# Twenty-four token blocks' normalised input transposed by 32 x 32 squares and DMA instead of by TensorE, and the squares carried through DRAM in pieces of 512 bytes

## The reference

```python
q = (x @ wq.T).reshape(b, s, H, HD)            # k and v alike; H, HD = 16, 32
q, k = apply_rope(q, inv_freq), apply_rope(k, inv_freq)
scores = einsum('bshd,bstd->bsht', q, k) / sqrt(HD)   # the heads of ONE token attend to each other
attn = einsum('bsht,bstd->bshd', softmax(scores), v).reshape(b, s, HIDDEN) @ wo.T
hidden = fwht(silu(x @ W1.T) * (x @ W3.T))            # FFN with 2048 hidden features
out = hidden @ W2.T
...
x = x + 0.5 * ffn(layernorm(x))
x = x + attn(layernorm(x))
x = x + 0.5 * ffn(layernorm(x))
```

## Time and profile before

| | |
|---|---|
| median of 3 runs | 2503.43 us (2501.75 to 2504.49) |
| the profiled execution | 2501.66 us, span 2499.8 us |
| PE busy | 2489.7 us (100%) |
| DVE busy | 2044.3 us (82%) |
| ACT busy | 530.2 us (21%) |
| POOL busy | 63.0 us (3%) |

### The profile page before, as it was taken

How to read it: one execution, slowest core, us unless ns; L and a number is a source line. 1 busy time by engine, 2 the same in 40 slices (tenths; PEclk the granted TensorE clock), 3 DMA queues, 4 the chain that set the end, 5 groups by cost and what they waited for, 6 DMA issues and landing times.

```text
span 2499.8 us, 30169 instructions
## 1 busy us (share of the span) xinstructions
PE 2489.7 (100%) x11111; PEld 2061.4 (82%) x11111; DVE 2044.3 (82%) x2602; ACT 530.2 (21%) x796; POOL 63.0 (3%) x109
## 2 busy tenths in 40 slices
PE   9999999999999999999999999999999999999999
PEld 7878888888888888888888888888888888888887
DVE  9569989699786997979969899797986979878711
ACT  3332212222121221222212122122121212211211
POOL 0030000000000000000000000000000000000000
PEclk9999999999999999999999999999999999999999
DMA  9645635455352564645635466454562545535364
GB/s 343 254 188 181 218 145 200 131 202 210 135 201 81 210 216 162 224 131 206 207 109 188 168 229 208 146 220 144 202 221 93 197 148 219 190 107 199 137 219 165
DMA packets 161172, 459.48 MB, mean 184 GB/s; under 512 B 53312, under 2 KB 82240, under 8 KB 127808
## 3 DMA queue, kind: packets, MB, share of 16 engines
q1 hardware_dynamic: 81792, 419.73, 46.0%
q10 hardware_dynamic: 79296, 38.68, 5.7%
HBM read 408.04 MB, written 38.80 MB: 179 GB/s over the span
## 4 chain that ended last, share of the span: by engine, by line
PE 90%; DVE 8%; issue 1%; DMA 0%; ACT 0%; POOL 0%; SPq 0%; DVEq 0%; ACTq 0%; POOLq 0%
PE gu L608 19%; PE gu L610 19%; PE gu L609 19%; PE acc L639 8%; PE acc L640 8%; PE acc L643 8%; PE acc L608 2%; PE acc L610 2%; PE acc L609 2%; DVE scores L1323 1%; DVE mixed L1325 1%; DVE prod L1316 1%; DVE prod L1311 1%; PE acc L736 1%; DVE gated L1584 1%
## 5 line engine op out<-in xcount | busy, mean ns | idle before, releaser
L608 PE MATMUL gu<-xt,w_up 128*128 128x512 f32 x2048 | 798.4, 390 | 0.2
L610 PE MATMUL gu<-xt,w_up 128*128 128x512 f32 x2048 | 796.8, 389 | 0.0
L609 PE MATMUL gu<-xt,w_up 128*128 128x512 f32 x2048 | 796.7, 389 | 0.0
L608 PEld LDWEIGHTS gu<-xt,w_up 128*128 128x128 f32 x2048 | 384.4, 188 | 80.7 <-issue 0.8
L609 PEld LDWEIGHTS gu<-xt,w_up 128*128 128x128 f32 x2048 | 384.4, 188 | 80.0
L610 PEld LDWEIGHTS gu<-xt,w_up 128*128 128x128 f32 x2048 | 384.4, 188 | 79.8
L1584 DVE TENSOR_TENSOR gated<-gated,gu 128x512 f32<-128x512 f32 x240 | 162.8, 679 | 239.8 <-PE gu L610 238.3
L639 PE MATMUL acc<-w_down,hid 128*128 128x512 f32 x896 | 349.6, 390 | 0.0
L640 PE MATMUL acc<-w_down,hid 128*128 128x512 f32 x896 | 348.6, 389 | 0.0
L1084 ACT ACTIVATE hid<-gated 128x512 fp32r<-128x512 f32 x240 | 152.0, 633 | 892.2 <-DVE gated L1584 882.6
L1325 DVE TENSOR_REDUCE mixed<-prod 128x64 f32<-128x1024 f32 x256 | 310.1, 1213 | 0.0
(11 more groups left out here) (144 smaller groups left out, 1946.8 us busy)
## 6 DMA issues: line engine op xcount, KB each, us to landing
w_up<-up_pairs SPq DMA_DIRECT2D x240, 1024.0 KB, 4.9
w_down<-down_pairs SPq DMA_DIRECT2D x240, 512.0 KB, 3.5
up_pairs<-w_up SPq DMA_DIRECT2D x16, 1024.0 KB, 5.1
xt<-tok ACTq DMA_DIRECT2D x176, 64.0 KB, 4.1
prod<-up_raw SPq DMA_DIRECT2D x16, 512.0 KB, 6.3
down_pairs<-w_attn SPq DMA_DIRECT2D x4, 2048.0 KB, 18.4
out<-x ACTq DMA_DIRECT2D x7, 1024.0 KB, 5.3
x<-x ACTq DMA_DIRECT2D x6, 1024.0 KB, 6.5
```

The costliest lines, as they stand in the source:

```text
L608: nc.tensor.matmul(o, w_hi, m_hi, start=first, stop=False)
L609: nc.tensor.matmul(o, w_hi, m_lo, start=False, stop=False)
L610: return nc.tensor.matmul(o, w_lo, m_hi, start=False, stop=last)
```

## The change

Block inputs take the way of the squares: the 24 early blocks are normalised in step 11, in the order of 32-feature groups that the later steps want, transposed in place on VectorE in 32 x 32 squares, kept in DRAM (`sub_squares`, step 12), brought back by 4 DMAs of 64 KB a block (steps 13 and 14), and split from SBUF (step 15). The FFN input's squares go to DRAM too (`tile_squares`, one DMA in step 10) and come back by 4 DMAs of 256 KB in step 11; its high part moves from step 14 to step 13. The attention outputs are brought back in pieces of 512 bytes into `turned`, and the split puts them in order. On ScalarE the DMA issues now stand ahead of `EXP_BEHIND`. `units_by_step` counts the new work as 1.25 a block in step 11, for 0.55 in step 13. In the prologue GpSimd's low part of the output weights waits for two ropes.

```diff
-X_STATS, X_APPLY, X_MOVE, X_SPLIT, Q_STATS, Q_APPLY = 6, 8, 10, 14, 10, 13
+X_STATS, X_APPLY, X_KEEP, X_MOVE, X_SPLIT = 6, 8, 10, 11, 13
+Q_STATS, Q_APPLY, Q_KEEP, Q_MOVE, Q_SPLIT = 10, 11, 12, 13, 15
...
-    beside[Q_APPLY] += 0.55 * len(early_subs(p + 1))
+    beside[Q_APPLY] += 1.25 * len(early_subs(p + 1))
...
             def query_key(g, between=None):
-                split_ready("q", g, 0)
+                if g in MOVED_SUBS:
+                    pe.wait_ge(s_sub_lo, MOVED_SUBS[g] + 1)
+                else:
+                    split_ready("q", g, 0)
...
             def late_gap(p):
-                output(p, 0)
-                output(p, 1)
-                if new:
-                    pe.wait_ge(s_added, SUBS * p)
-                    transpose_sub(new[0])
-                    transpose_sub(new[1])
-                output(p, 2)
-                output(p, 3)
+                for s in range(SUBS):
+                    output(p, s)
...
-                    pe.wait_ge(s_h, n0 + HT - 1)
-                    for g in early_subs(after):
-                        transpose_sub(g)
                     down_step(last, 0, False, False)
...
-            def move(p, q):
+            def keep_squares(p):
                 act.wait_ge(s_turned, SUBS * MOVED[p] + SUBS)
-                squares = turned.rearrange("p (k f c) -> p k f c", k=KT, f=QUADS)
+                act.dma_start(tile_squares, turned).then_inc(s_squares_kept, 16)
+
+            def move(p):
+
+                act.wait_ge(s_squares_kept, 16 * MOVED[p] + 16)
+                squares = tile_squares.rearrange("(q i) (k f c) -> f i k q c", q=QUADS, k=KT, f=QUADS)
                 for f in range(QUADS):
-                    act.dma_start(xt[p % 2][32 * f:32 * f + 32, 1].bitcast(FP32)[:, :, q * P:(q + 1) * P],
-                                  squares[32 * q:32 * q + 32, :, f, :]).then_inc(s_moved, 16)
+                    act.dma_start(xt[p % 2][32 * f:32 * f + 32, 1].bitcast(FP32).rearrange("p k (q c) -> p k q c", q=QUADS),
+                                  squares[f]).then_inc(s_moved, 16)
...
+            def keep_sub_squares(g):
+                act.wait_ge(s_sub_turned, MOVED_SUBS[g] + 1)
+                act.dma_start(sub_squares[new_subs(next_of(g)).index(g)], sub_normed(g)).then_inc(s_sub_kept, 16)
+
+            def move_sub(g):
+
+                later = max(early_subs(next_of(g)))
+                act.wait_ge(s_sub_kept, 16 * MOVED_SUBS[later] + 16)
+                squares = sub_squares[new_subs(next_of(g)).index(g)].rearrange("(q i) (f c) -> f i q c", q=QUADS, f=QUADS)
+                for f in range(QUADS):
+                    act.dma_start(sub_normed(g)[32 * f:32 * f + 32, :].rearrange("p (q c) -> p q c", q=QUADS),
+                                  squares[f]).then_inc(s_sub_moved, 16)
+
+            def moved_sub_high(g):
+                later = max(early_subs(next_of(g)))
+                act.wait_ge(s_sub_moved, 16 * QUADS * (MOVED_SUBS[later] + 1))
+                high = sub_split(g)[0].rearrange("p k (q j) -> p k q j", q=QUADS)
+                nc.scalar.activation(high, landed_sub(g), ACT.Copy).then_inc(s_sub_hi, 1)
...
                 act.wait_ge(s_att_kept, 16 * SUBS * (BOUNCED[i] + 1))
-                act.wait_ge(s_up_done, HT * p)
...
-                    act.dma_start(xt[(p + 1) % 2][32 * f:32 * f + 32, 1].bitcast(FP32).rearrange("p k (a j) -> p k a j", j=32),
+                    act.dma_start(turned[32 * f:32 * f + 32, :].rearrange("p (a c) -> p a c", c=P),
                                   squares[f]).then_inc(s_att_moved, 16)
...
                     nc.scalar.activation(hidden(u)[0], gated[:, u, :], ACT.Copy).then_inc(s_hid_hi, 1)
-                    if n == HT - 1 and after < NP and after not in LATE:
+                    for g in OUTPUT_KEEP.get((p, n), ()):
+                        keep_output(g)
+                    if after in MOVED and n == X_KEEP:
+                        keep_squares(after)
+                    if after in MOVED and n == X_MOVE:
+                        move(after)
+                    if after < NP and n == Q_KEEP:
                         for g in early_subs(after):
-                            sub_high(g)
+                            keep_sub_squares(g)
+                    if after < NP and Q_MOVE <= n < Q_MOVE + len(early_subs(after)):
+                        move_sub(early_subs(after)[n - Q_MOVE])
                     for g in EXP_BEHIND.get((p, n), ()):
                         exp(g)
-                    for g in OUTPUT_KEEP.get((p, n), ()):
-                        keep_output(g)
-                    if after in MOVED and X_MOVE <= n < X_MOVE + QUADS:
-                        move(after, n - X_MOVE)
                     if after in MOVED and n == X_SPLIT:
                         moved_high(after)
+                    if after < NP and n == Q_SPLIT:
+                        for g in early_subs(after):
+                            moved_sub_high(g)
...
             for m in range(4):
                 for k in range(KT):
+                    if m == O and k == 0:
+                        pool.wait_ge(s_rope, 2)
...
+            def moved_sub_low(g):
+                dve.wait_ge(s_sub_hi, MOVED_SUBS[g] + 1)
+                high, low = [part.rearrange("p k (q j) -> p k q j", q=QUADS) for part in sub_split(g)]
+                nc.vector.tensor_tensor(low, landed_sub(g), high.bitcast(FP32), ALU.subtract).then_inc(s_sub_lo, 1)
...
                         if n == Q_APPLY:
+                            if after in MOVED:
+                                dve.wait_ge(s_turned, SUBS * MOVED[after] + SUBS)
                             for s, g in enumerate(early):
-                                ln_apply(key, s, sub_normed(g), x_of(g))
+                                ln_apply(key, s, sub_normed(g).rearrange("p (f k j) -> p k f j", f=QUADS, k=KT),
+                                         x_of(g).rearrange("p (k f j) -> p k f j", f=QUADS, k=KT))
+                            for s, g in enumerate(early):
+                                dve.wait_ge(s_ln, ln_done(key, s))
+                                squares = sub_normed(g).rearrange("p (f j) -> p f j", j=32)
+                                nc.vector.transpose(squares, squares).then_inc(s_sub_turned, 1)
...
                     if n == HT - 1 and next_x:
                         for g in early:
-                            sub_low(g)
+                            moved_sub_low(g)
```

More of the change, by code:

```diff
@@ L89 @@
 UNITS = units_by_pass()
-X_STATS, X_APPLY, X_MOVE, X_SPLIT, Q_STATS, Q_APPLY = 6, 8, 10, 14, 10, 13
+X_STATS, X_APPLY, X_KEEP, X_MOVE, X_SPLIT = 6, 8, 10, 11, 13
+Q_STATS, Q_APPLY, Q_KEEP, Q_MOVE, Q_SPLIT = 10, 11, 12, 13, 15
 STEPS = HT - 1
 MOVED = {p: at for at, p in enumerate(p for p in range(2, NP) if p not in LATE)}
+MOVED_SUBS = {g: at for at, g in enumerate(g for p in range(2, NP) for g in early_subs(p))}
 QUADS = P // 32
@@ L173, in transposed @@
         elif p in LATE:
-            order += att + [("q", g, 0) for g in new[:2]] + [("x", p, k) for k in range(KT)]
+            order += att + [("x", p, k) for k in range(KT)]
         else:
-            order += [("q", g, 0) for g in early_subs(p)]
             order += [("q", g, 0) for j, g in enumerate(new[:2]) if not is_early(p, j)] + att
@@ L362, in build @@
         s_moved_lo = sem("s_moved_lo")
+        s_sub_turned = sem("s_sub_turned")
+        s_sub_kept = sem("s_sub_kept")
+        s_sub_moved = sem("s_sub_moved")
+        s_sub_hi = sem("s_sub_hi")
+        s_sub_lo = sem("s_sub_lo")
         s_att_turned = sem("s_att_turned")
@@ L458, in sub_normed, with landed_sub, landed_outputs @@
             return prod[:, 2, (j % 2) * D:(j % 2 + 1) * D]
+        def landed_sub(g):
+            return sub_normed(g).rearrange("p (q k j) -> p k q j", q=QUADS, k=KT)
+        def landed_outputs():
+            return turned.rearrange("p (a k j) -> p k a j", j=32, k=KT)
         def sub_split(g):
@@ L787, in late_gap @@
                     query_key(new[0])
-                    split_ready("q", new[1], 0)
                 pe.wait_ge(s_ln, LN_FROM["x", p] + SUBS)
@@ L952, in moved_high, with next_of @@
                     nc.scalar.activation(X[:, 0, ks, :], X[:, 1, ks, :].bitcast(FP32), ACT.Copy).then_inc(s_moved_hi, 1)
+            def next_of(g):
+                return next(p for p in range(2, NP) if g in new_subs(p))
+            def keep_sub_squares(g):
[13 more added lines that the diff above has]
+                nc.scalar.activation(high, landed_sub(g), ACT.Copy).then_inc(s_sub_hi, 1)
             def keep_output(g):
@@ L970, in moved_attention_high @@
                 act.wait_ge(s_att_moved, 16 * QUADS * (BOUNCED[WO_AT[p]] + 1))
-                X = xt[(p + 1) % 2]
+                act.wait_ge(s_up_done, HT * p)
                 for ks in (slice(0, 2), slice(2, 4)):
-                    nc.scalar.activation(X[:, 0, ks, :], X[:, 1, ks, :].bitcast(FP32), ACT.Copy).then_inc(s_att_hi, 1)
```

(11 more changed lines are left out.)

20 lines of the change are left out of this document (15 added, 5 removed).

## The result

| | before | after |
|---|---|---|
| median, 20 executions each | 2502.46 us (2501.51 to 2504.49) | 2507.41 us (2500.78 to 2511.66) |
| ratio, 95% interval | | 1.0016 [1.001, 1.0022] |
| profiled execution, span | 2501.66, 2499.8 us | 2505.99, 2504.2 us |

What follows compares the result with a forecast made beforehand. TensorE's own work was taken as the bound nearly everywhere. Pass ends 3.9 plus prologue 2.2 made 6.1 us gained, moving the median from 2503.4 to 2497.3 us; range 2494 to 2500.5, with rivals 2490.5 to 2502.7.

Steps and rivals of the forecast that it cites:

- TensorE is the bound, and two blocks' transposes are worth 0.89 us: At pass ends, removing two blocks' transposes saves TensorE 0.89 us; at most 10.7 us for all 24 blocks.
- my 0.8: Ends of passes 3, 7 and 9: 0.8 us gained each, 2.4 in all, with slightly more delay on VectorE.
- The prologue's 2.2: Prologue: with GpSimd's work behind two ropes, block 0's rope ends earlier and TensorE's wait goes, 2.2 us gained.
- Passes 1 and 10: 0: Ends of passes 1 and 10: TensorE arrives 0.45 us earlier at the normalised block and waits 0.45 longer, gaining 0.
- ScalarE ... has 79% idle, so this costs only where something late stands behind them; bounds 0 and 2.55: ScalarE's DMA issues in steps 10 to 14: cost between 0 and 2.55 us for each of passes 2 and 6.
- Pass 2 was to gain 0.77: End of pass 2: `moved_high` goes to step 13, so VectorE's 0.77 us wait for the last SiLU goes.
- A move takes 4.1 ... to land: hidden.: A block's move, issued in step 14 and needed some 13 us later, lands in 4.1 us and costs nothing.
- a wait at `query_key`: Sign against the forecast: TensorE waiting at the gap's query and key projections would show it wrong; no size given.
- Passes 5, 6 and 8: Ends of these passes: planner's new deal brings VectorE 1.35 us later to step 15; 0.45, 1.95 and 0.45 us lost.
- The forms and pieces cost nothing: Reordered operations on bounced tiles and fewer output pieces cost nothing; about 1 us over passes 5, 6, 8 as other bound.
- the second: Rival: VectorE's backlog and ScalarE's issues, reaching the low part in passes 2 and 6, eat the gain; 2502.3 us, chance 0.20.
- The third: Rival: squares land too late for the gap's first query projection, 4.4 us lost at 13 pass ends; 2554 us, chance 0.07.

Runs made afterwards that it cites:

- e6: The changed kernel with the FFN input's moves issued behind the SiLU of step 12 and both blocks' behind that of step 14: 2497.56 us, ratio 0.9979.
- e8: The changed kernel without VectorE's 24 square transposes of blocks, so their features come in a wrong order: 2494.97 us, ratio 0.9971.
- e3: The changed kernel with the attention units dealt to the steps as in the kernel before: 2502.53 us, ratio 1.0002.
- e4: The changed kernel with twelve needless matmuls ahead of the last down projection of passes 2 and 6: 2503.19 us, ratio 1.0.
- e9: The kernel before with only the attention outputs' part of the change, pieces of 512 bytes and the reordering split: 2503.09 us, ratio 1.0001.

## Why the prediction was wrong

By its own steps:

- **TensorE is the bound, and two blocks' transposes are worth 0.89 us.** Right: passes 4, 12 and 13 gained 0.90, 0.87 and 0.93. Pass 3 kept 0.66 and pass 9 0.30 for my 0.8; in 9 the low part ended 2.90 behind the up projection, where 12 matmuls cover 2.6.
- **The prologue's 2.2.** Right (2.13; alone 2.00).
- **Passes 1 and 10: 0.** Right.
- **"ScalarE ... has 79% idle, so this costs only where something late stands behind them; bounds 0 and 2.55".** This step failed. The bound was that of the issues' own duration. It left out that the first move of a block waits for a landing in DRAM, 13.6 us behind its issue in pass 2, and that all of ScalarE's program waits with it. Pass 2 was to gain 0.77 and lost 4.53. e6 puts the issues behind the SiLU, and pass 2 gains 0.83. That the landing took 13.6 is this execution's; with 10.6 and 10.9 (e8, e3) the pass lost nothing.
- **"A move takes 4.1 ... to land: hidden."** Failed in passes 5, 8 and 11, where it took 5 to 9 beside w_up's load; the median over all moves was as priced (3.8), and the price should have been that of the slow ones. I had worked out that a landing is free until X + 4.4, and took X - 5.2 for the issue. In pass 8 the second block's was issued at 1413.91, which is X - 4.0 (X, the end of the up projection, is 1417.9), and had landed at 1424.0, X + 6.2. I had named a wait at `query_key` as what would prove me wrong, and it did.
- **Passes 5, 6 and 8.** The sizes were right: low parts at 3.70 and 5.77 where the forecast's numbers give 3.7 and 5.8. The reason was not. I had put it on the planner's deal; e3 leaves the low part where it is, and e8 shows that it is the two transposes' own 1.2 us on an engine without idle time.
- **What a wait costs.** I priced it by its length. Behind waits of 3.25 and 3.20 us the clock was at half, 2.6 and 1.6 us more. That is the rest of the error in passes 2 and 6; for pass 6, e4 removes it in one execution.
- **The forms and pieces cost nothing.** Right (e9).

Of the rivals, the second was nearest: it had ScalarE's issues reach the low part in passes 2 and 6, but only by the issues' own duration, and the result is 5 us slower still. The third had the right wait, the squares coming late, but not its usual place: only passes 5, 8 and 11 met it, by 0.4 to 0.7 us.

**Open:** how late a landing is differs from execution to execution, so medians and accounts of single profiles disagree by a few microseconds (the changed kernel's executions lie between 2500.8 and 2511.7), and the place of a loss in one profile isn't its mean. What sets a landing's length wasn't tried. That the w_up load beside it sets the block moves' 7.2 us was argued from the issue times, not tried.

## What to carry to other kernels

A DMA issue that first waits for another DMA stalls everything behind it in its engine's program, however idle that engine is; put it where the engine has just finished what others wait for, and price the wait by the slowest landing in the trace, not by the median. When work moves from the bound to an engine with 18% idle, look for the stretches in which that engine has none, and move other work out of them in the same edit: with both, the same change was worth 11 us (0.45%) in place of a loss of 5. Behind a long wait of TensorE, count on more: in 19 of the 21 waits of 2.2 to 4.5 us here, a third to four fifths of the wait was lost again in clock.

## What was unexpected of the hardware

- **The clock behind a wait.** Over all fourteen traces here, from the prologue's gap on, 21 waits made a distance between two of TensorE's matmuls 2.2 to 4.5 us longer than usual. Behind 19 of them 5 to 12 matmuls came at 0.427 us in place of 0.227 (1.3 to 2.7 us lost); behind two, 3.32 us in e6 and 2.39 in the kernel before, none did. Behind 20 such delays of 1.2 to 2.0 us none came slow, unless one of the long waits followed first.
- **Landings in DRAM.** In the changed kernel's trace the blocks' 256 KB from SBUF to DRAM landed in 3.8 to 13.6 us (median 6.4) and the FFN input's 1 MB in 4.9 to 8.9; 64 KB back in 1.8 to 8.7. The Trainium skill ("DMA: Bandwidth & Descriptors", section "Latency and other measured facts") has 2 us for access to HBM at high load as the main part of a fixed cost. The landings here were up to several times that. The DMA share was 1.04 from 435 to 449 us, over the longest of them, and 0.89 from 1413 to 1424.
- **Issue time.** One of a block's four moves takes 0.45 us of ScalarE's sequencer (1.81 for four), and eight of them (3.99) cost nothing where ScalarE waits for VectorE until 451.94 anyway (e6). The four of the FFN input took 2.6 to 4.05 us.
